# The second layer of a graph network: scalars of x spread by DMA and contracted in one go

## The chip, the cores and the metric

The kernel runs on one core of a Trainium2 chip. The metric is the device time of one execution in microseconds, as a median over runs. The engines are PE (TensorE), DVE (VectorE), ACT (ScalarE), POOL (GpSimd) and SP (SyncE, which here only issues DMAs).

## What is computed

Two layers of a message-passing network over 12500 nodes and 200000 edges, each followed by a layer norm. A node has 160 features: 64 scalars and 32 vectors of three components. The change is in the node update of the second layer:

```
a0, a1 = agg[:, :64], agg[:, 64:].reshape(n, 32, 3)      # sum of the messages at each node
xs, xv = x[:, :64], x[:, 64:].reshape(n, 32, 3)
u0 = einsum('nu,nv,uvw->nw', xs, a0, Wu_ss) * INV64 + einsum('nui,nvi,uvw->nw', xv, a1, Wu_vv) * (INV_SQRT3 * INV32)
u1 = (einsum('nu,nvi,uvw->nwi', xs, a1, Wu_sv) + einsum('nui,nv,uvw->nwi', xv, a0, Wu_vs)) * INV_SQRT2048
u0 = u0 + xs @ Lu_s * INV8
u1 = u1 + einsum('nui,uw->nwi', xv, Lu_v) * INV_SQRT32
x = layernorm(x + x + concat(u0, u1))                    # the layer adds x, and the caller adds x again
```

The first term of u0, with a weight of 64 x 64 x 64, is the one that the change computes in another way. All of it is in f32.

## The kernel before

The program has three stages. The first sorts the edges by their source node and makes the first layer's messages. The second is the first layer's sweep over 100 tiles of 125 nodes, which also makes the second layer's messages. The third is the second layer's sweep over the same tiles (`node_sweep`, `node_step` with `layer == 1`), some 1800 of the 6805 us. There is no scheduler: each engine runs its list as it is written, and they wait for each other on semaphores. A step t sums the messages of tile t (`edges`) and updates tile n = t - 1 (`nodes`). So the engines' work in a step of the second layer is, in each one's order:

- PE: `bilinear(0..5)`, of which 0 to 3 make scalar products into prods_ps (L1301, L1302: 64 rows each, the two halves of the array), each of the two buffers in turn, and 4 and 5 make the mixed products (L1304, L1305); `sum_edges`, the product of the one-hot matrix with the messages (L1352, 17 blocks) and the spilled rows (L1353); `turn_q(0)` (L1339); `scalar_sums`, which adds up zs by products with a band matrix, four groups of 32 columns at a time (L1320); `turn_q(1)`; `turn_y`, which turns the aggregate (a2) and x (x2, v) (L1382 to L1384); `linear`, which adds the linear part, the products of q with w_vv (L1369) and the turned scalars (L1371) in m_ps. An f32 product shows as two records.
- DVE: `scalars(0..3)` multiplies the scalar products by the turned x (zs, L1034), `mixed_mul` (L1071), `mixed_sum` (L1084), then the residual, 2 x on top of m_ps (L1115), and h (L1117).
- ACT: `prods_out` copies the mixed products for POOL (L1593), `deviation` (L1537 to L1543), `features` (L1582 to L1584), `summed` (L1608, L1609), `turned_q(0)` (L1601), `scalars_out` (ss_t, L1636), `turned_q(1)`, `turned_y` (L1626 to L1628), `normal` (L1553), and `one_hot` for the next tile (L1701, L1707).
- POOL: its third of the mixed products (L757), then q of tile t (L731, L766).
- SP: the load of x (L562), of the next tile's messages (msgs, L377) and spilled rows (L588), the stores of out (L397, L398).

PE's edge sum of tile t waits for ACT's one-hot matrix (`hot`); ACT's `summed` waits for the edge sum; POOL's q and the turn of y wait for `summed`. The matrix has one buffer, so that ACT builds it only after the edge sum before.

Of the kernel before, what the change touches and what calls it, by code (L numbers as in the profile page):

```python
# [13 lines left out]
P = 128  # L14
# [44 lines left out]
RS_ALL = R0 + R1 + 1  # L59
# [9 lines left out]
USES = [R0 + d * R1 for d in DIRECT]  # L69


def used(layer, r):

    return r + 1 if r < R0 else R0 + DIRECT[layer] * (r + 1 - R0)
# [23 lines left out]
def build(nc, x, src, dst, attr, weights, out):  # L98
# [37 lines left out]
    x_mid = nc.dram_tensor("x_mid", [N, D], F32).ap()  # L136
    picks_d = nc.dram_tensor("picks", [UNITS, P, UB * P], F32).ap()
    recs_d = nc.dram_tensor("edge_recs", [P, NCH, CB * REC], F32).ap()

    with ExitStack() as whole:  # L140
# [21 lines left out]
        in_order = sb("in_order", [P, S])  # L162
        ones_f = sb("ones_f", [P, P])
# [97 lines left out]
        row_id = q3[:, 0:NCOL]  # L261

# [18 lines left out]
        dma_go, sp_go, edges_clear = sem("dma_go"), sem("sp_go"), sem("edges_clear")  # L281
# [5 lines left out]
        def layer_sems(layer):  # L287
            s = {}
            for n in ("hot", "edges_done", "y_out", "y_turned", "y_turned_out", "prods", "prods_used", "upd", "q_mul", "q_part", "ss_out",
                      "q_turned", "q_turned_out", "lin", "lin_out", "h_ready", "deviation", "inverse", "normed",  # L290
                      "msg", "pay_out", "located",
                      "t_turned", "t_turn_out", "t_mm", "t_out", "first_fill",
                      "sp_ids", "sp_link", "sp_index", "sp_rec", "sp_keys", "sp_tab", "sp_sum", "sp_old", "sp_put", "sp_done"):
                s[n] = sem(f"{n}_l{layer}")
            for n in (("picked", "pick_turned", "pick_out"), ("copied", "mixed_mul"))[layer]:
                s[n] = sem(f"{n}_l{layer}")
            for n in ("msgs_in", "x_in", "stored", "spill_in", "rec_in", "t_stored", "filled"):
                s[n] = [sem(f"{n}{b}_l{layer}") for b in range(2)]
            for n in ("win_in", "scattered"):
                s[n] = [sem(f"{n}{q}_l{layer}") for q in range(4)]  # L300
# [24 lines left out]

        def later(k):
# [23 lines left out]
        def _(sp):  # L350
            def carry():
                sp.sem_inc(sp_go, 1)
# [69 lines left out]
            def load_node_weights(layer):  # L422
# [4 lines left out]
                ss_halves = w["u_ss"].rearrange("v (r h c) -> h v r c", h=2, c=512)  # L427
# [38 lines left out]
            def load_recs(layer, k):  # L466
                c, ck, cb = k
                s = LS[layer]
                if within(c, 2, NCH):
                    if layer == 0:  # L470
# [3 lines left out]
                             ).then_inc(s["rec_in"][cb], 16)  # L474
# [78 lines left out]
            def node_step(layer, k, chunk):  # L553
# [12 lines left out]
                if layer == 1 and within(t, 0, NT - 1):  # L566
# [4 lines left out]
                    load_spilled(layer, later(k))  # L571
                if within(t, 2, NT + 2):
# [10 lines left out]
                if layer == 0 and within(t, 2, NT + 2):  # L583
                    store_table(1, (t - 2, half - 1, b))

            def load_spilled(layer, k):
                t, half, b = k
                sp.dma_start(spill_in[b][:, :], spill_sums[layer][bass.ds(t * HM, P), :]).then_inc(LS[layer]["spill_in"][b], 16)  # L588

            for layer in range(2):  # L590
                s = LS[layer]
                if layer == 1:
                    for b in range(2):
                        sp.wait_ge(LS[0]["stored"][b], 32 * (NT // 2))
                first_msgs(layer)
# [1171 lines left out]
```

## Time and profile before

| what | us |
|---|---|
| time, median of 3 runs (6799.92 to 6801.0) | 6800.83 |
| the profiled execution's own time | 6806.87 |
| its span, first to last instruction | 6805.1 |
| PE busy | 5627.2 (83%) |
| DVE busy | 5466.6 (80%) |
| POOL busy | 5272.0 (77%) |
| ACT busy | 3741.2 (55%) |

The busy shares are means over stages with different limits, so that a change in one stage is read from that stage alone: the stretches of time of the rows below. A record of PE's matmuls shows when it started; records overlap, and a row with a count spans them all. An idle time in brackets is that of the engine just before the row, with what ended it.

### The profile page before, as it was taken

To read this page: it belongs to the slowest core of one execution; us is meant where nothing else is said; L and a number is where in the kernel's file an instruction comes from. 1 tells how busy PE (TensorE), PEld (TensorE's weight loads), DVE (VectorE), ACT (ScalarE), POOL (GpSimd) and SP (SyncE) were. 2 spreads that over 40 slices of the span, in tenths; PEclk is the share of its full clock that TensorE was granted. 3 is DMA by queue.
4 is the path that set the end of the run, shared out by engine and by line. 5 is a ranking of instruction groups with operands and counts; after the bars stand their busy time and mean duration, and the time that the engine had idled before them with its cause. 6 is when DMAs were issued, how large, how long until landed. Compare 5 with 4: busy or idle time off the path is not lost.

```text
span 6805.1 us, 145388 instructions
## 1 busy us (share of the span) xinstructions
PE 5627.2 (83%) x52295; PEld 4582.1 (67%) x52295; DVE 5466.6 (80%) x7299; ACT 3741.2 (55%) x11578; POOL 5272.0 (77%) x4099
## 2 busy tenths in 40 slices
PE   5566666666664799999999999999589999999998
PEld 3455555545554577777777777777467777877877
DVE  6777777777775788888888888888378988998998
ACT  2333333333332566666666666666267777777776
POOL 2777777777777478888888888888768788888887
PEclk6787878888887899999999999999799999999999
DMA  7888888888884377878787878787422222222222
GB/s 222 258 259 259 257 258 263 255 259 256 257 257 145 122 259 261 261 259 262 257 262 256 264 256 263 254 266 255 140 92 93 92 96 98 92 93 101 92 92 74
DMA packets 681148, 1380.99 MB, mean 203 GB/s; under 512 B 106047, under 2 KB 487661, under 8 KB 654447
## 3 DMA queue, kind: packets, MB, share of 16 engines
q1 hardware_dynamic: 527695, 1090.23, 51.0%
q0 software_dynamic: 152736, 281.45, 12.2%
q8 instruction: 418, 6.85, 0.4%
q14 instruction: 299, 2.45, 0.1%
HBM read 587.20 MB, written 784.08 MB: 202 GB/s over the span
## 4 chain that ended last, share of the span: by engine, by line
PE 43%; POOL 16%; DMA 10%; DVE 9%; issue 8%; SPq 8%; ACT 6%; POOLq 0%; DVEq 0%; ACTq 0%
POOL slots L647 12%; PE node_ps L1352 8%; PE prods_ps L1301 8%; DMA slots<-pay,slot_all 5%; DVE zs L1034 4%; PE prods_ps L1304 3%; PE prods_ps L1320 3%; POOL q L704 3%; DMA rec<-edge_recs 3%; PE node_ps L1369 3%; PE m_ps L1369 2%; PE turn_ps L1339 2%; ACT onehot L1701 2%; PE s_ps L1217 2%; SPq L346 2%
## 5 line engine op out<-in xcount | busy, mean ns | idle before, releaser
L647 POOL DMA_INDIRECT slots<-pay,slot_all x3136 | 3263.7, 1041 | 1023.9 <-issue 786.6
L1701 ACT ACTIVATE onehot<-node_iota,msgs 128x125 f32<-128x125 f32 x3400 | 1030.5, 398 | 122.1 <-POOLq L691 122.1
L1352 PEld LDWEIGHTS node_ps<-msgs,onehot 128*125 128x125 f32 x6800 | 932.5, 188 | 139.3 <-issue 98.5
L1352 PE MATMUL node_ps<-msgs,onehot 128*125 128x160 f32 x6800 | 981.1, 303 | 35.8 <-ACT onehot L1707 25.2
L1084 DVE TENSOR_REDUCE upd<-work 125x48 f32<-125x3072 f32 x300 | 1004.0, 3347 | 6.8
L1217 PE MATMUL m_ps<-win,picks_sb 125*128 125x160 f32 x3136 | 666.5, 341 | 390.9 <-ACT pay L1502 381.5
L1071 DVE TENSOR_TENSOR work<-prods_ps,yv 125x1024 f32<-125x1024 f32 x800 | 931.4, 1217 | 64.3 <-PE prods_ps L1305 63.4
L1217 PEld LDWEIGHTS m_ps<-win,picks_sb 125*128 125x128 f32 x3136 | 525.2, 217 | 478.8 <-issue 379.7
L731 POOL TENSOR_TENSOR q<-xt,yv 125x3072 f32<-125x3072 f32 x100 | 547.6, 5476 | 340.4 <-PE turn_ps L1339 322.9
L1034 DVE TENSOR_TENSOR zs<-prods_ps,x_t 128x1000 f32<-128x1000 f32 x400 | 469.6, 1196 | 133.8 <-PE prods_ps L1302 133.8
L1487 ACT COPY picks_sb<-s_ps 125x512 f32<-125x512 f32 x392 | 229.8, 586 | 594.8 <-PE s_ps L1199 521.0
L1034 DVE TENSOR_TENSOR zs<-prods_ps,spill_tab 128x1000 f32<-128x1000 f32 x400 | 469.6, 1196 | 90.2 <-PE prods_ps L1302 90.1
L704 POOL TENSOR_TENSOR q<-xt,yv 125x512 f32<-125x512 f32 x400 | 451.3, 1130 | 94.6 <-PE turn_ps L1339 69.8
L766 POOL TENSOR_TENSOR q<-q 125x1024 f32<-125x1024 f32 x200 | 473.0, 2365 | 15.7
L1301 PE MATMUL prods_ps<-a_t,w_bil 64*128 64x125 f32 x3200 | 439.7, 281 | 22.9 <-DVE zs L1034 20.9
L1301 PE MATMUL prods_ps<-spill_tab,w_bil 64*128 64x125 f32 x3200 | 439.9, 281 | 21.2 <-DVE zs L1034 21.1
L1302 PE MATMUL prods_ps<-spill_tab,w_bil 64*128 64x125 f32 x3200 | 457.3, 284 | 0.0
L1302 PE MATMUL prods_ps<-a_t,w_bil 64*128 64x125 f32 x3200 | 457.0, 284 | 0.0
L1707 ACT ACTIVATE onehot<-onehot,ones_f 128x1375 f32<-128x1375 f32 (+2 forms) x300 | 443.8, 1479 | 3.4
L1185 PE MATMUL prods_ps<-bucket_onehot,after_bf 128*128 128x500 bf16 x392 | 171.0, 436 | 330.1 <-DVE bucket_onehot L900 329.7
L1502 ACT COPY pay<-m_ps 128x320 f32<-128x320 f32 x784 | 331.3, 423 | 185.1 <-PE m_ps L1217 183.0
L1301 PEld LDWEIGHTS prods_ps<-a_t,w_bil 64*128 64x128 f32 x3200 | 385.6, 187 | 63.3 <-DVE zs L1034 31.6
(273 smaller groups left out, 13494.3 us busy)
## 6 DMA issues: line engine op xcount, KB each, us to landing
msgs<-slots SPq DMA_DIRECT2D x200, 1428.0 KB, 6.4
slots<-zero SPq DMA_DIRECT2D x183, 1386.0 KB
win<-table SPq DMA_DIRECT2D x784, 160.0 KB
picks<-picks_sb SPq DMA_DIRECT2D x196, 512.0 KB
picks_sb<-picks SPq DMA_DIRECT2D x196, 512.0 KB
table<-tab SPq DMA_DIRECT2D x200, 350.0 KB
slots<-pay,slot_all POOLq DMA_INDIRECT x3136
spill_in<-spill_sums SPq DMA_DIRECT2D x200, 80.0 KB, 6.0
```

Of the source, the lines that this page charges most:

```text
L647: g.indirect_dma_start(out=slots[layer][:, :], out_offset=bass.IndirectOffsetOnAxis(ap=slot_all[:, j:j + 1], axis=0), in_=pay[q][:, j - UB ...
L704: g.tensor_tensor(q3[0:HM, VV * i + V * u0:VV * i + V * u0 + VV // 2].rearrange("p (u v) -> p u v", v=V), xt[nb][0:HM, S:D].rearrange("p ( ...
L731: g.tensor_tensor(q3[0:HM, VV * i0:].rearrange("p (i u v) -> p i u v", u=V, v=V), xt[nb][0:HM, S:D].rearrange("p (u i) -> p i u", i=3)[:, ...
L766: add = g.tensor_tensor(q3[0:HM, 0:VV], q3[0:HM, 0:VV], q3[0:HM, VV * (j + 1):VV * (j + 2)], ALU.add)
L1034: ve.tensor_tensor(zs[:, r, :, :, :], prods_ps[(nb + r) % 2][:, :].rearrange("p (h c) -> p h c", h=2)[:, :, 0:QUARTER * HM].rearrange("p h ...
L1071: ve.tensor_tensor(wk[:, i, :, :].rearrange("p w (h k) -> p h w k", h=2), prods_ps[(nb + r) % 2][0:HM, :].rearrange("p (h w k) -> p h w k" ...
L1084: ve.tensor_reduce(upd1[:, :, w0:w0 + ROUND // KV], mixed_part(r), AX_X, ALU.add).then_inc(s["upd"], 1)
L1217: mm = te.matmul(to[:, D * j:D * j + D], (pick_b[q] if layer else pick_n[hh])[0:WROWS, P * (2 * p + j):P * (2 * p + j) + P], win[q][0:WROW ...
L1301: te.matmul(to[:, HM * q:HM * q + HM], w.bil[0:S, o:o + P], a2_t[nb][0:S, :], start=True, stop=True)
L1302: mm = te.matmul(to[:, 512 + HM * q:512 + HM * q + HM], w.bil[S:P, o:o + P], a2_t[nb][S:P, :], start=True, stop=True)
L1352: te.matmul(node_ps[0:HM, 0:D], onehot[:, j, :], msgs[b][:, j, 0:D], start=(j == 0), stop=False)
L1701: last = ac.activation(onehot[:, j, :], node_iota[:, :], ACT.Square, bias=msgs[b][:, j, LOCAL:LOCAL + 1], scale=-1.0)
```

## The change

In the second layer the term with Wu_ss is computed from products that are made ahead of the matmul. The first layer's sweep writes the turned scalars of its result to HBM (x0_t, one DMA for each tile). In the second layer SP loads them spread over partitions: partition v of each half holds, for 8 values of u, the row x[u, 125 nodes], the same in all 64 partitions (`spread_x`: four pieces z, two DMAs of 64 x 4000 bytes for each). DVE multiplies each piece in place by the turned aggregate, which it reads from PSUM (`spread_scaled`). PE contracts the 128 rows (u half and v) with the weights of 64 columns, 32 products which alternate between the two halves of the columns and accumulate in node_ps (`scalar_products`); the vv products follow in the same form into the same sum (`vector_products`). ACT copies that sum as ss_t, and one product with `folded` (two identity matrices, one above the other) adds the halves to m_ps. The residual 2 x goes into the linear weights (`ident2` is twice the identity), and the operation for it on DVE is gone. Three of the four pieces have two buffers (in zs, and in parts of pay and picks that the second layer leaves free), the fourth has one. Some semaphores are shared between the layers to make room; the first layer's step is otherwise as before, but for the store of x0_t and a wait of ACT for it ahead of its next copy into ts_t.

The core of the diff:

```
 DVE
+                def spread_scaled(z):
+                    ve.wait_ge(s["y_turned_out"], 3 * n + 3)
+                    if z == 0:
+                        ve.wait_ge(s["xs_in"][nb], 32 * (SPREAD - 1) * (nh + 1))
+                    if z == SPREAD - 1:
+                        ve.wait_ge(s["xs_last"], 32 * n + 32)
+                    ve.tensor_tensor(xs[nb][z][:, :, :], xs[nb][z][:, :, :], s_ps[:, 2 * HM:3 * HM].unsqueeze(1).broadcast_to([P, PER, HM]),
+                                     ALU.mult).then_inc(s["scaled"], 1)
...
-                    for r in range(R0):
-                        scalars(r)
+                    for z in range(SPREAD):
+                        spread_scaled(z)
...
-                    if layer == 1:
-                        ve.scalar_tensor_tensor(m_ps[0:HM, 0:D], xt[nb][0:HM, :], 2.0, m_ps[0:HM, 0:D], ALU.mult, ALU.add).then_inc(s["lin_out"], 1)
-                        ve.wait_ge(s["lin_out"], n + 1)
 PE
+                def scalar_products():
+                    if not nodes:
+                        return
+                    te.wait_ge(s["y_out"], Y_OUT * min(t + 1, NT))
+                    for z in range(SPREAD):
+                        te.wait_ge(s["scaled"], SPREAD * n + z + 1)
+                        for r in range(PER):
+                            o, half_of = S * (PER * z + r), S * (r % 2)
+                            mm = te.matmul(node_ps[half_of:half_of + S, 0:HM], w.bil[:, o:o + S], xs[nb][z][:, r, :],
+                                           start=(z == 0 and r < 2), stop=False, tile_position=(0, half_of))
+                        mm.then_inc(s["scaled_used"], 1)
+                def vector_products():
+                    if not nodes:
+                        return
+                    te.wait_ge(s["q_turned_out"], 2 * n + 2)
+                    for j in range(QC):
+                        half_of = S * (j % 2)
+                        mm = te.matmul(node_ps[half_of:half_of + S, 0:HM], w.vv[:, j, :], q_t[:, j, :],
+                                       start=False, stop=(j >= QC - 2), tile_position=(0, half_of))
+                    mm.then_inc(s["out0"], 1)
...
-                    for r in range(SUMS):
+                    for r in range(R0, SUMS):
                         bilinear(r)
                     sum_edges()
                     turn_q(0)
-                    scalar_sums()
+                    scalar_products()
                     turn_q(1)
                     turn_y()
+                    vector_products()
                     linear()
 ACT
-                    ac.wait_ge(s["prods"], RS_ALL * n + RS_ALL)
+                    ac.wait_ge(*((s["ss_prods"], n + 1) if layer == 0 else (s["out0"], n + 1)))
...
                     turned_q(0)
-                    scalars_out()
                     turned_q(1)
                     turned_y()
+                    scalars_out()
                     normal()
 SP
+                if layer == 1 and within(t, 0, NT):
+                    for z in range(SPREAD):
+                        spread_x(k, z)
...
+                    sp.dma_start(x0_t[t - 2], ts_t[:, :]).then_inc(LS[1]["x_put"], 16)
+            def spread_x(k, z):
+                t, half, b = k
+                s = LS[1]
+                behind = 2 if z < SPREAD - 1 else 1
+                if within(t, behind, NT):
+                    sp.wait_ge(s["scaled_used"], SPREAD * (t - behind) + z + 1)
+                for hh in range(2):
+                    frm = x0_t[t, S // 2 * hh + PER * z:S // 2 * hh + PER * (z + 1), :].rearrange("u n -> (u n)")
+                    sp.dma_start(xs[b][z][S * hh:S * hh + S, :, :].rearrange("p r n -> p (r n)"), frm.unsqueeze(0).broadcast_to([S, PER * HM])
+                                 ).then_inc(s["xs_in"][b] if z < SPREAD - 1 else s["xs_last"], 16)
```

ACT's list in a step of the second layer, from the first copy of q_t to the copies of the mixed products of the next step. Before:

```order
L1601 COPY q_t<-turn_ps 128x500 [waits lin_l1,q_turned_l1]
L1636 COPY spill_tab<-prods_ps 128x125 [waits lin_l1,prods_l1]
L1601 COPY q_t<-turn_ps 128x500 [waits q_turned_l1]
L1626 COPY spill_tab<-s_ps 128x125 [waits lin_l1,y_turned_l1]
L1627 COPY spill_tab<-s_ps 128x125
L1628 COPY spill_tab<-s_ps 96x125
L1553 ACTIVATE res<-centred,stats 125x160 [waits stored1_l1,inverse_l1]
L1701 ACTIVATE onehot<-node_iota,msgs 128x125 [waits edges_done_l1,msgs_in0_l1]
L1701 ACTIVATE onehot<-node_iota,msgs 128x125 x16
L1707 ACTIVATE onehot<-onehot,ones_f 128x2125 [waits squared1]
L1593 COPY pay<-prods_ps 125x1024 [waits mixed_mul_l1,prods_l1] x2
```

And now, the same place:

```order
L1682 COPY q_t<-turn_ps 128x500 [waits out0_l1,q_turned_l1]
L1682 COPY q_t<-turn_ps 128x500 [waits q_turned_l1]
L1707 COPY spill_tab<-s_ps 128x125 [waits lin_l1,y_turned_l1]
L1708 COPY spill_tab<-s_ps 128x125
L1709 COPY spill_tab<-s_ps 96x125
L1717 COPY spill_tab<-node_ps 128x125 [waits lin_l1,out0_l1]
L1634 ACTIVATE res<-centred,stats 125x160 [waits stored1_l1,inverse_l1]
L1782 ACTIVATE onehot<-node_iota,msgs 128x125 [waits edges_done_l1,msgs_in0_l1]
L1782 ACTIVATE onehot<-node_iota,msgs 128x125 x16
L1788 ACTIVATE onehot<-onehot,ones_f 128x2125 [waits squared1]
L1674 COPY pay<-prods_ps 125x1024 [waits mixed_mul_l1,prods_l1] x2
```

The copy of the scalars (L1636, now L1717) went from between the two copies of q_t to just ahead of the normalisation, and waits for `out0`, which PE signals behind the vv products.

PE's list in a step of the second layer, from the turn of y to the turn of q, before (the scalar products of the bilinear part, 32 rows of L1301 and L1302, are left out between the pieces):

```order
L1384 MATMUL s_ps<-ident,yx 96x125
L1366 MATMUL m_ps<-w_lin_u,v_t 125x96 [waits h_ready_l1,q_turned_out_l1]
L1367 MATMUL m_ps<-w_lin,x_t 125x64
L1369 MATMUL m_ps<-w_vv,q_t 125x64 x8
L1371 MATMUL m_ps<-in_order,spill_tab 125x64 [waits ss_out_l1]
L1301 MATMUL prods_ps<-spill_tab,w_bil 128x125 [waits copied_l1,prods_used_l1,y_turned_out_l1]
L1302 MATMUL prods_ps<-spill_tab,w_bil 128x125
```

And now, from the turn of y to the turn of q:

```order
L1462 MATMUL s_ps<-ident,yx 96x125
L1394 MATMUL node_ps<-q_t,w_vv 64x125 [waits q_turned_out_l1]
L1394 MATMUL node_ps<-q_t,w_vv 64x125 x7
L1441 MATMUL m_ps<-w_lin_u,spill_tab 125x96 [waits h_ready_l1]
L1442 MATMUL m_ps<-w_lin,spill_tab 125x64
L1447 MATMUL m_ps<-folded,spill_tab 125x64 [waits ss_out_l1]
L1356 MATMUL prods_ps<-w_bil,x_t 125x512 [waits copied_l1,prods_used_l1,y_turned_out_l1]
L1357 MATMUL prods_ps<-w_bil,a_t 125x512
L1356 MATMUL prods_ps<-w_bil,x_t 125x512 [waits copied_l1,prods_used_l1,y_turned_out_l1]
L1357 MATMUL prods_ps<-w_bil,a_t 125x512
L1426 MATMUL node_ps<-msgs,onehot 125x160 [waits y_out_l1,spill_in1,hot_l1]
L1426 MATMUL node_ps<-msgs,onehot 125x160 x16
```

Between the linear part and the edge sum stood 32 scalar products and the four mixed ones; now the four mixed ones alone do, and the edge sum with its wait for `hot` comes right behind them.

## Rows read from the trace of the kernel before

**Rows 1.** Stretches: us, busy us (records) of PE, PEld, DVE, ACT, POOL, PEclk, DMA, GB/s

```profile
3500.00:4600.00 1100.00, 1051.70 (x10338) 853.96 (x10338) 932.02 (x720) 700.15 (x2371) 914.33 (x845) 1.00 0.80 259
5000.00:6700.00 1700.00, 1611.78 (x19053) 1355.19 (x19052) 1529.43 (x1208) 1280.54 (x3534) 1380.56 (x465) 1.00 0.28 95
```

**Rows 2.** PE's timeline in one step: start us, us, engine, line, operation, tiles

```profile
6038.06 4.88 PE L1352 MATMUL node_ps<-msgs,onehot 128*125 128x160 f32 x34
...
6046.73 0.46 PE L1366 MATMUL m_ps<-w_lin_u,v_t 96*125 96x96 f32 x2 [0.35 <-ACT q_t L1601]
...
6054.19 0.69 PE L1304 MATMUL prods_ps<-w_bil,spill_tab 64*125 64x512 f32 x1 [0.20 <-DVE zs L1034]
...
6056.36 4.88 PE L1352 MATMUL node_ps<-msgs,onehot 128*125 128x160 f32 x34
```

**Rows 3.** Chain of waits in the second layer: start us, us, what

```profile
6043.22 0.43 PE turn_ps L1339 x4
6043.64 1.84 PE prods_ps L1320 x64
6045.48 0.59 PE turn_ps L1339 x4
...
6047.38 1.75 PE m_ps L1369 x16
6049.12 0.22 PE m_ps L1371 x2
```

**Rows 4.** Waits, 5100 to 6600 us: who for whom, us in total, times, longest us

```profile
PE prods_ps L1301 <- DVE zs L1034: 33.5, 82, 0.4
```

**Rows 5.** ACT in the same step, its timeline

```profile
6045.55 0.26 ACT L1636 COPY spill_tab<-prods_ps 128x125 f32<-128x125 f32 x1 [1.29 <-PE prods_ps L1320]
...
6046.88 0.28 ACT L1628 COPY spill_tab<-s_ps 96x125 f32<-96x125 f32 x1
6047.04 0.45 ACT L1553 ACTIVATE res<-centred,stats 125x160 f32<-125x160 f32 x1
6047.37 5.03 ACT L1701 ACTIVATE onehot<-node_iota,msgs 128x125 f32<-128x125 f32 x17
6052.43 2.07 ACT L1707 ACTIVATE onehot<-onehot,ones_f 128x2125 f32<-128x2125 f32 x1
```

**Rows 6.** A gap of PE in the sort: its timeline, and stretches of 1 us

```profile
493.45 0.39 PE L1185 MATMUL prods_ps<-bucket_onehot,after_bf 128*128 128x500 bf16 x1 [4.62 <-DVE bucket_onehot L900]
...
493.00:494.00 1.00, 0.55 (x4) 0.34 (x5) 0.96 (x3) 0.00 (x0) 0.74 (x1) 0.99 0.96 279
494.00:495.00 1.00, 1.00 (x8) 0.98 (x6) 0.93 (x3) 0.00 (x0) 0.96 (x1) 0.50 0.61 196
...
497.00:498.00 1.00, 1.00 (x4) 0.29 (x2) 0.95 (x2) 0.00 (x0) 0.70 (x2) 0.81 1.08 404
```

**Rows 7.** The first two edge sums of the second layer, timeline, and a stretch

```profile
4959.54 7.74 PE L1352 MATMUL node_ps<-msgs,onehot 128*125 128x160 f32 x34 [11.06 <-ACT onehot L1707]
...
4976.42 4.88 PE L1352 MATMUL node_ps<-msgs,onehot 128*125 128x160 f32 x34
...
4959.00:4965.00 6.00, 5.46 (x20) 5.49 (x21) 0.00 (x0) 1.06 (x4) 0.00 (x0) 0.50 0.00 0
```

**Rows 8.** DVE's groups, 5000 to 6700 us: busy us, mean ns, idle before

```profile
L1034 DVE TENSOR_TENSOR zs<-prods_ps,spill_tab 128x1000 f32<-128x1000 f32 x184 | 212.3, 1196 | 20.1 <-PE prods_ps L1302 20.1
L1115 DVE SCALAR_TENSOR_TENSOR m_ps<-xt,m_ps 125x160 f32<-125x160 f32 x93 | 30.7, 330 | 12.8 <-DVE upd L1084 0.5
```

**Rows 9.** DMA issues, 5100 to 6600 us (KB, us to landing), and SP's timeline

```profile
msgs<-slots SPq DMA_DIRECT2D x82, 1428.0 KB, 6.4
...
6050.60 0.43 SPq L377 DMA_DIRECT2D msgs<-slots  x1
```

**Rows 10.** SP's waits in the first layer's sweep, 3000 to 4500 us

```profile
SPq L397 <- ACT tab L1476: 716.4, 58, 13.6
```

**Rows 11.** The last edge sum, PE's timeline

```profile
6770.06 4.88 PE L1352 MATMUL node_ps<-msgs,onehot 128*125 128x160 f32 x34
```

More of the change, by code:

```diff
@@ L68, with used @@
 DIRECT = (3, 2)
-USES = [R0 + d * R1 for d in DIRECT]
-def used(layer, r):
-    return r + 1 if r < R0 else R0 + DIRECT[layer] * (r + 1 - R0)
+USES = [R0 + DIRECT[0] * R1, DIRECT[1] * R1]
+SPREAD = 4
+PER = S // 2 // SPREAD
+def used(r):
+    return r + 1 if r < R0 else R0 + DIRECT[0] * (r + 1 - R0)
 def row_sum(r, half):
@@ L324, in within, with recs_by @@
             return not isinstance(k, int) or lo <= k < hi
+        def recs_by(layer, ck):
+            return 16 * (NCH // 2 * layer + ck + 1)
         def later(k):
@@ L1345, in sum_edges @@
                     te.wait_ge(s["hot"], t + 1)
-                    te.wait_ge(s["spill_in"][b], 16 * half + 16)
+                    te.wait_ge(spill_in_by[b], 16 * (NT // 2 * layer + half + 1))
                     if layer == 0 and within(t, 2, NT):
@@ L1357, in linear @@
                         return
-                    te.wait_ge(s["q_turned_out"], 2 * n + 2)
-                    if layer == 0 and edges:
-                        te.wait_ge(s["y_out"], Y_OUT * t + Y_OUT)
-                    if layer == 1 and within(n, 1, NT):
+                    if layer == 0:
+                        te.wait_ge(s["q_turned_out"], 2 * n + 2)
+                        if edges:
+                            te.wait_ge(s["y_out"], Y_OUT * t + Y_OUT)
+                    elif within(n, 1, NT):
                         te.wait_ge(s["h_ready"], n)
@@ L1367, in linear @@
                     te.matmul(to[0:HM, 0:S], x2_t[nb][:, :], w.lin0[:, :], start=layer == 1, stop=False)
-                    for j in range(QC):
-                        te.matmul(to[0:HM, 0:S], q_t[:, j, :], w.vv[:, j, :], start=False, stop=False)
+                    if layer == 0:
+                        for j in range(QC):
+                            te.matmul(to[0:HM, 0:S], q_t[:, j, :], w.vv[:, j, :], start=False, stop=False)
                     te.wait_ge(s["ss_out"], n + 1)
-                    te.matmul(to[0:HM, 0:S], ss_t[:, :], in_order[:, :], start=False, stop=True).then_inc(s["lin"], 1)
+                    te.matmul(to[0:HM, 0:S], ss_t[:, :], (in_order, folded)[layer][:, :], start=False, stop=True).then_inc(s["lin"], 1)
                 def turn_y():
@@ L1458, in table_turned @@
                     ac.wait_ge(s["t_mm"], m)
+                    if layer == 1:
+                        ac.wait_ge(s["x_put"], 16 * m)
                 ac.copy(ts_t[:, :], turn_ps[0:S, 0:HM])
@@ L1589, in prods_out @@
                         return
-                    ac.wait_ge(s["prods"], RS_ALL * n + R0 + j + 1)
+                    ac.wait_ge(s["prods"], R1 * n + j + 1)
                     if within(n, 1, NT):
                         ac.wait_ge(s["mixed_mul"], R1 * n - R1 + j + 1)
-                    ac.copy(prods_sb[j][0:HM, :], prods_ps[(nb + R0 + j) % 2][0:HM, :]).then_inc(s["copied"], 1)
+                    ac.copy(prods_sb[j][0:HM, :], prods_ps[(R0 + j) % 2][0:HM, :]).then_inc(s["copied"], 1)
                 def turned_q(part):
@@ L1632, in scalars_out @@
                         return
-                    ac.wait_ge(s["prods"], RS_ALL * n + RS_ALL)
+                    ac.wait_ge(*((s["ss_prods"], n + 1) if layer == 0 else (s["out0"], n + 1)))
                     if within(n, 1, NT):
                         ac.wait_ge(s["lin"], n)
-                    ac.copy(ss_t[:, :], prods_ps[(nb + SUMS) % 2][:, 0:HM]).then_inc(s["ss_out"], 1)
+                    ac.copy(ss_t[:, :], (prods_ps[(nb + SUMS) % 2] if layer == 0 else node_ps)[:, 0:HM]).then_inc(s["ss_out"], 1)
                 def normal():
@@ L1731, with laid_out @@
 }
-def laid_out(name, a):
+def laid_out(name, a, layer):
+    if name == "u_ss" and layer == 1:
+        return np.ascontiguousarray(a.transpose(1, 0, 2).reshape(S, SS))
     if name in ("u_ss", "u_vs"):
```

115 lines of the change are left out of this document (69 added, 46 removed).

## The prediction

> **What bounds the kernel now.** I read by stage first [rows 1]. In the stretch from 5000 to 6700 us, which is the second layer's sweep over the nodes, PE is busy 1611.78 of 1700 us, at the full granted clock (1.00), with VectorE (DVE) at 1529.43 behind it; the DMA engines have a share of 0.28 and move 95 GB/s. Only this stage and its loads are touched by most of the change. One step of it is one tile of 125 nodes, and from one edge sum to the next are 6056.36 - 6038.06 = 18.30 us [rows 2]. The chain of waits runs through PE block after block [rows 3], and the longest wait of a PE matmul for another engine is 0.4 us [rows 4].
>
> So a reader may think: take PE work away, and DVE with 1529.43 / 1700 x 18.30 = 16.5 us a step is next. That is only so if no other closed loop is longer than 16.5 us, and the trace of ScalarE (ACT) shows one that now has little slack. In ACT's order the one-hot matrix of the next tile (L1701, L1707) stands behind the copies of this step, runs from 6047.37 to 6052.43 + 2.07 = 6054.50 [rows 5], and PE's edge sum (L1352) waits for it. The next edge sum begins at 6056.36: the one-hot was ready 1.86 us early. The loop edge sum, products, copies, one-hot, next edge sum is thus 18.30 - 1.86 = 16.4 us long today.
>
> **The change part by part.** *PE work.* The 32 bilinear products of 64 rows go, the 64 band records (L1320, 1.84 us) go, and what replaces both is 32 products of 128 rows and 64 columns, f32, thus 64 records, which alternate between the two column halves. No row has this form. The nearest are the band sums: 64 records, four column groups side by side, 1.84 / 16 = 0.115 us for each group of four [rows 3]. With two side by side I take 32 x 0.115 = 3.68 us. The bounds are 1.84 (a record costs the same as there) and 64 x 0.115 = 7.36 (no overlap). I take 3.68, since the moving side has the same 125 columns as the band sums. They stand in the step where the band sums stood, between the two turns of q. The eight vv products change their form likewise: 16 records in pairs, 8 x 0.115 = 0.92 us (bounds 0.46 and 1.84; 1.75 now [rows 3]), and they move out of the linear part to ahead of it.
>
> *ACT's order.* This is the term that decides. ss_t was copied early, between the two copies of q_t, and is now copied behind turned_y from the sum that also holds the vv products. So the scalars' copy, the normalisation, and the one-hot behind it on ACT all wait until PE has done its vv products. New loop, from an edge sum's start: to the start of the scalar products 6043.64 - 6038.06 = 5.58; scalar products 3.68; second turn of q 0.59 [rows 3]; from its end (6045.48 + 0.59 = 6046.07) over ACT's copy of q_t to the first PE instruction that waits for it, 6046.73: 0.66 [rows 2]; vv products 0.92; PE's end to ACT's copy 0.07 (6045.48 to 6045.55), copy to normalisation 0.16 (6046.88 to 6047.04), normalisation to one-hot 0.33 (to 6047.37), together 0.56; one-hot 7.13 [rows 5]; 0.05 for the signal to PE. Sum 19.17 us. That is 0.87 over the present 18.30, although PE has less to do.
>
> *PE's gap and its clock.* From the end of the vv products PE has the linear part left, 6047.38 - 6046.73 = 0.65 and 0.22 of the last product [rows 3], and the mixed products, 6056.36 - 6054.19 = 2.17 [rows 2]. Then it stands until the one-hot is ready: 0.56 + 7.13 - 0.65 - 0.22 - 2.17 = 4.65 us in every step, where its longest wait is 0.4 now. What such a gap does is in the stage of the sort: after 4.62 us without a matmul the granted clock went from full to 0.50, the 1.2 GHz level, and it stayed there from the slice at 494 us through 0.19 / 0.50 = 0.38 of the one at 497, 3.38 us in which PE was busy [rows 6]. At half speed that costs 1.69 us. The edge sum itself shows the far end: behind a long gap, at 0.50, its 34 records took 7.74 us, and 4.88 in the next step [rows 7]: 2.86 us. In the new loop the work right behind the gap is this edge sum, on the path. Bounds 0 (the clock holds) and 2.86; I take 1.69, the gap of the same length. Step: 19.17 + 1.69 = 20.86 us.
>
> *Switches.* The second turn of q takes 0.59 us and the first 0.43, for the same four records [rows 3]: 0.16 us go where the column groups change. The change adds one such place on the loop, ahead of the vv products: up to 0.16 us a step, 98 x 0.16 = 16 us in all. I leave it out of the sum, since the 0.59 that I took already holds one such fill and the block ahead of the vv products is only three turns long, and keep it for the range (19.17 + 0.16 = 19.33). The Trainium skill (TensorEngine Tiling, Key Properties) says that a change of tiling mode drains the engine; by that rule the 16 us would be paid in full, and the 0.16 of the trace agrees with it.
>
> *DVE.* Four zs products of 1000 elements (1196 ns each) become four products in place, one input from PSUM as now; the 330 ns of the residual (L1115) go [rows 8]. So 16.5 - 0.3 = 16.2 us a step. In a step of 20.86 this is hidden; each new product could take 1 us more before DVE set the pace. They wait for the loads and for y_turned; queued behind them are the mixed products, and those wait for ACT's copies of prods_ps, which stand behind the one-hot, so that DVE too idles in the middle of its step. h then follows the linear part, 0.87 us behind the vv products, and PE asks for it a whole step later.
>
> *Loads.* Each step brings 8 DMAs of 64 x 4000 bytes, 2.05 MB, beside the present 95 GB/s x 18.30 us = 1.74 MB. 3.79 MB at the 259 GB/s that the first layer's sweep moves [rows 1] take 14.6 us, under the step. On SP's queue they stand behind the msgs load and ahead of the stores of out and of the next step's loads; 8 x 0.43 [rows 9] is 3.4 us of issue, where SP issues five DMAs a step now. The one-hot needs msgs a step later, which lands in 6.4 us [rows 9]. The fourth piece has one buffer and waits for PE's last scalar product; SP then waits for normed anyway. Price nothing; if the rate were half, 29 us a step.
>
> *The first layer.* One DMA of 32 KB a step on SP, which waits 716.4 us in 58 steps for the table there [rows 10], and a wait of ACT for that DMA a step later: nothing. The fold matrix and the residual in the weights are made once: nothing.
>
> **Sum.** The last edge sum of the sweep begins at 6770.06, the second at 4976.42 [rows 7, 11]: 98 steps of 18.30. 98 x (20.86 - 18.30) = 251 us. The profiled execution takes 6806.87 us (span 6805.1), 6 us above the median of 6800.83; 6806.87 + 251 - 6 = 7052 us.
>
> **Rivals.** (a) *The clock holds at 1.00.* Then the step is 19.17: 98 x 0.87 = 85, thus 6886. For it: the whole sweep is at 1.00 now. Against it: [rows 6]. (b) *Faster.* A record of the new products starts as often as a band record, whatever the number of column halves: scalar products 1.84, vv products 0.46, loop 16.87, and PE's clock holds; 98 x (16.87 - 18.30) = -140, thus 6661, DVE close behind. It decides from the point at which both blocks together take under 4.60 - 0.87 = 3.73 us. For it: records of 29 ns exist [rows 3]. Against it: there four column groups run at once, here two, and the gap for the clock stays. (c) *The two halves do not run side by side.* Blocks of 7.36 and 1.84, step 19.17 + 4.60 = 23.77, thus 7337 with the clock at full and 7503 with the price of the gap. The band sums speak against it, and the Trainium skill (TensorEngine Tiling, Available Configurations and Key Properties) lists 128 x 64 as two tiles that work in parallel; no row here shows it. (d) *The loads set the pace* with many reads of the same bytes: 29 us a step, 7850.
>
> **How the numbers follow.** The forecast, the loop over ACT with a fall of the clock, has 0.72 and reaches from 6930 to 7190 (step 19.6 to 22.2, that is up to 19.33 + 2.86). (a) has 0.12, (b) 0.06, (c) 0.04, (d) 0.04, and 0.02 are left for a step that comes out as now. The range takes in the forecast and (a): 6860 to 7190. Faster by over 0.2% is (b), 0.06; within 0.2% 0.04, the 0.02 and part of (a); slower 0.90. 0.2% is about what a measurement of this kernel can tell from no change.
>
> **What would show it.** Right: PE idle some 4.6 us ahead of each edge sum, released by ACT's one-hot; granted clock under 1.00 in the sweep, with edge sums of 6 to 8 us; steps near 20.9 us; scalar products 3.7 us at full clock; DVE below 85% busy. (a) shows a clock of 1.00 and steps of 19.2; (b) blocks of 1.84 and 0.46; (c) blocks of 7.4; (d) DVE waiting for loads at its first product. The prediction is wrong if ACT's one-hot does not end last ahead of the edge sum.

## The result, and the profile after

The changed kernel takes 7100.77 us (median of 4 runs, 7098.47 to 7103.29) where the kernel before takes 6800.91 beside it: a ratio of 1.044, 95% interval 1.0422 to 1.0458. It is 300 us slower; forecast were 251 us. The profiled execution took 7103.29 us, its span 7101.6.

By stages first, as in [rows 1]: us, busy us (records) of PE, PEld, DVE, ACT, POOL, granted clock, DMA share, GB/s, after the change.

```profile
3500.00:4600.00 1100.00, 1051.78 (x10336) 853.92 (x10334) 932.19 (x719) 699.82 (x2367) 914.12 (x845) 1.00 0.80 261
5000.00:6700.00 1700.00, 1268.67 (x11263) 1093.37 (x11261) 1272.14 (x958) 1079.17 (x3029) 1180.63 (x398) 0.88 0.63 177
```

The first layer's sweep is what it was. In the second layer's sweep every engine is busy for less of the time, PE 75% where it was 95%, and the clock granted to PE is 0.88 where it was 1.00. No engine is the bound; something closes a loop. PE's timeline of one step shows where (line numbers of the changed kernel: L1426 is the edge sum, L1383 the scalar products, L1394 the vv products, L1356 the mixed products). It answers [rows 2].

```profile
6019.35 6.95 PE L1426 MATMUL node_ps<-msgs,onehot 128*125 128x160 f32 x34 [5.00 <-ACT onehot L1788]
...
6027.06 1.93 PE L1383 MATMUL node_ps<-pay,w_bil 128*64 128x125 f32 x32
...
6031.94 1.08 PE L1394 MATMUL node_ps<-q_t,w_vv 128*64 128x125 f32 x16 [0.35 <-ACT q_t L1682]
6032.95 0.46 PE L1441 MATMUL m_ps<-w_lin_u,spill_tab 96*125 96x96 f32 x2
...
6033.75 0.69 PE L1356 MATMUL prods_ps<-w_bil,x_t 64*125 64x512 f32 x1
...
6035.14 0.59 PE L1356 MATMUL prods_ps<-w_bil,x_t 64*125 64x512 f32 x1
...
6040.73 0.63 PE L1426 MATMUL node_ps<-msgs,onehot 128*125 128x160 f32 x1 [5.00 <-ACT onehot L1788]
```

This step lasts 6040.73 - 6019.35 = 21.38 us (18.30 before). The bracket is the reading that matters: PE stood still for 5.00 us ahead of the edge sum, and ACT's one-hot matrix ended that wait; the longest wait before was 0.4 [rows 4]. The view of waits (us in total, times, longest us) from 5100 to 6500 us says that this is so in every step (66 steps, 5.0 us each). DVE does not wait for a load anywhere; its waits are one ahead of its mixed products (L1124) and one ahead of h, for the linear part (L1447):

```profile
PEld node_ps L1426 <- ACT onehot L1788: 384.9, 66, 5.8
PE node_ps L1426 <- ACT onehot L1788: 330.1, 66, 5.0
...
DVE picks_sb L1124 <- issue: 202.6, 66, 3.4
DVE h L1167 <- PE m_ps L1447: 150.2, 65, 3.3
```

For L1124 the view names no releaser. By the kernel it waits for ACT's copy L1674, which stands behind the one-hot in ACT's list, and the timelines of the two engines fit that, since DVE starts as the first of the two copies ends:

```profile
6040.59 1.91 ACT L1674 COPY pay<-prods_ps 125x1024 f32<-125x1024 f32 x2
6041.67 1.23 DVE L1124 TENSOR_TENSOR picks_sb<-prods_ps,yv 125x1024 f32<-125x1024 f32 x1 [3.06 <-issue]
```

The chain of waits (start us, us, what), to be set against [rows 3], runs through ACT for over a third of the step:

```profile
6019.35 6.95 PE node_ps L1426 x34
...
6027.06 3.64 PE node_ps L1383 x64
6030.70 0.59 PE turn_ps L1413 x4
6031.31 0.59 ACT q_t L1682
...
6031.94 1.10 PE node_ps L1394 x16
...
6033.23 0.43 ACT res L1634
6033.65 4.93 ACT onehot L1782 x17
6038.61 2.08 ACT onehot L1788
```

And the clock, in stretches of 1 us around the end of the gap (columns as above; the clock is the third number from the end):

```profile
6039.00:6040.00 1.00, 0.00 (x0) 0.00 (x0) 0.00 (x0) 1.00 (x1) 0.92 (x2) 1.00 0.95 400
6040.00:6041.00 1.00, 0.27 (x1) 0.27 (x2) 0.00 (x0) 1.00 (x2) 1.00 (x1) 0.83 0.92 312
6041.00:6042.00 1.00, 1.00 (x5) 1.00 (x6) 0.33 (x1) 1.00 (x2) 1.00 (x2) 0.50 0.98 230
...
6044.00:6045.00 1.00, 1.00 (x9) 1.00 (x8) 1.00 (x2) 0.73 (x4) 1.00 (x2) 0.96 1.03 244
```

As PE resumes it falls to 0.50, the 1.2 GHz level, and is back at 2.4 GHz three to four us later. The edge sum stands in just that stretch: over the steps from 5100 to 6450 us its 34 records take 6.27 to 7.83 us, 6.89 in the mean, where every one took 4.88 before.

### The profile page after: what moved, and what is told of

Read it like the earlier page. It is cut to its first block, busy times and chain, and to the rows that moved or that the text cites. A ratio compares the mean times of both kernels' runs of the same rounds, so it can differ in the third digit from the quotient of the medians.

```text
span 7101.6 us, 133589 instructions
## 1 busy us (share of the span) xinstructions
PE 5478.5 (77%) x45895; PEld 4487.5 (63%) x45895; DVE 5415.4 (76%) x7200; ACT 3721.0 (52%) x11578; POOL 5268.9 (74%) x4099
## 4 chain that ended last, share of the span: by engine, by line
PE 38%; ACT 16%; POOL 16%; DMA 8%; issue 8%; SPq 8%; DVE 6%; POOLq 0%; DVEq 0%; ACTq 0%
POOL slots L682 13%; PE node_ps L1426 11%; ACT onehot L1782 9%; PE node_ps L1383 5%; PE prods_ps L1353 5%; DMA slots<-pay,slot_all 3%; ACT onehot L1788 3%; DMA rec<-edge_recs 3%; POOL q L739 3%; PE node_ps L1445 2%; PE s_ps L1267 2%; PE turn_ps L1413 2%; SPq L363 2%; SPq L389 2%; ACT q_t L1682 2%
## 5 line engine op out<-in xcount | busy, mean ns | idle before, releaser
L1426 PE MATMUL node_ps<-msgs,onehot 128*125 128x160 f32 x6800 | 1178.6, 341 | 530.7 <-ACT onehot L1788 520.1
L1426 PEld LDWEIGHTS node_ps<-msgs,onehot 128*125 128x125 f32 x6800 | 1130.0, 221 | 641.0 <-ACT onehot L1788 617.1
L1124 DVE TENSOR_TENSOR work<-prods_ps,yv 125x1024 f32<-125x1024 f32 x800 | 931.3, 1217 | 64.7 <-PE prods_ps L1357 63.4
L1124 DVE TENSOR_TENSOR picks_sb<-prods_ps,yv 125x1024 f32<-125x1024 f32 x200 | 235.6, 1220 | 303.9 <-issue 300.5
L1682 ACT COPY q_t<-turn_ps 128x500 f32<-128x500 f32 x400 | 228.6, 572 | 443.6 <-PE turn_ps L1413 441.6
L1689 ACT COPY xa<-node_ps 125x128 f32<-125x128 f32 x200 | 53.3, 267 | 737.7 <-PE node_ps L1427 737.7
L1107 DVE TENSOR_TENSOR q<-q 125x1024 f32<-125x1024 f32 x186 | 234.4, 1260 | 146.9 <-POOL q L739 146.9
L1249 PE MATMUL s_ps<-ident,picks_sb 128*125 128x128 f32 x1568 | 320.5, 338 | 22.0 <-ACT picks_sb L1568 18.4
L1137 DVE TENSOR_REDUCE upd<-picks_sb 125x48 f32<-125x3072 f32 x100 | 334.3, 3343 | 1.1 <-issue 1.1
L1267 PE MATMUL node_ps<-win,picks_sb 125*128 125x160 f32 x1568 | 330.2, 339 | 2.1 <-ACT pay L1583 2.0
```

Source lines behind the costliest of these rows:

```text
L1124: ve.tensor_tensor(wk[:, i, :, :].rearrange("p w (h k) -> p h w k", h=2), prods_ps[((nb if layer == 0 else 0) + r) % 2][0:HM, :].rearrange ...
L1137: ve.tensor_reduce(upd1[:, :, w0:w0 + ROUND // KV], mixed_part(r), AX_X, ALU.add).then_inc(s["upd"], 1)
L1267: mm = te.matmul(to[:, D * j:D * j + D], (pick_b[q] if layer else pick_n[hh])[0:WROWS, P * (2 * p + j):P * (2 * p + j) + P], win[q][0:WROW ...
L1426: te.matmul(node_ps[0:HM, 0:D], onehot[:, j, :], msgs[b][:, j, 0:D], start=(j == 0), stop=False)
L1682: ac.copy(q_t[:, QC // 2 * part:QC // 2 * (part + 1), :], turn_ps[:, 0:QC // 2 * HM].rearrange("p (c n) -> p c n", n=HM)).then_inc(s["q_tu ...
```

## The experiments

**Theory:** the closed loop edge sum, scalar products, vv products, ACT's copy and one-hot, next edge sum sets the step, and its gap on PE costs the clock on top. **Rivals:** the spread transfers or DVE set the pace; the edge sum is slow for another reason than the gap; the loop does not run over the copy of the scalars. Steps and edge sums are means over 5100 to 6450 us of each trace; times are medians, those of the kernel before beside them 6799 to 6803. Each trace is of one run, mostly within 4 us of the median; that of e2_vv_linear took 7013.71 us, that of e1_hot_early 6683.17 and that of e9_before_early 7190.18.

| kernel | time, us | ratio, 95% interval | step, us | edge sum, us | clock, 5100 to 6500 us |
|---|---|---|---|---|---|
| before | 6800.91 | 1 | 18.30 | 4.88 | 1.00 |
| changed | 7100.77 | 1.0422 to 1.0458 | 21.33 | 6.89 | 0.88 |
| e3_fill | 6908.43 | 1.0141 to 1.0175 | 19.33 | 4.88 | 1.00 |
| e4_few_loads | 7100.32 | 1.0424 to 1.0459 | 21.33 | 6.89 | 0.88 |
| e2_vv_linear | 6998.75 | 1.0272 to 1.0306 | 20.48 | 7.00 | 0.88 |
| e5_half_s | 7020.49 | 1.0300 to 1.0334 | 20.48 | 7.75 | 0.83 |
| e1_hot_early | 6693.00 | 0.9834 to 0.9867 | 17.11 | 4.99 | 0.93 |
| e7_msgs_early | 6575.74 | 0.9651 to 0.9683 | 15.97 | 4.88 | 1.00 |

**The clock by itself (e3_fill).** Products of no use in PE's gap; everything else as in the changed kernel:

```diff
+                    if nodes and edges:
+                        if within(n, 1, NT):
+                            te.wait_ge(s["h_ready"], n)
+                        for j in range(6):
+                            te.matmul(m_ps[0:HM, D:512], w.bil[:, 128 * j:128 * j + HM], w.bil[:, 1024:1024 + 512 - D], start=True, stop=True)
                     sum_edges()
```

> The changed kernel with six products of no use (128 x 125 weights, 352 columns, written to columns of a bank that nobody reads) put on TensorE between the mixed products and the edge sum, where it waits 5.0 us for the one-hot matrix; by columns against the 4.88 us of the edge sum's 18 products of 160 they last 6 x 0.59 = 3.5 us, so they fit in the gap. Theory (the clock falls because TensorE stands still in each step, and the slow edge sum then lies on the loop): granted clock over 0.97, edge sums 4.9 to 5.2 us instead of 6.3 to 7.8, step 19.2 to 19.6 us, time 7101 - 99 x 1.9 = 6910 us (6890 to 6950). Rival (edge sums are slow because of the loads' traffic or the operands, or the clock falls for the sum of work): edge sums stay over 6 us, 7090 to 7140 us. Were the products themselves on the path, the time would rise by up to 3.5 x 99 = 350 us.

6908.43 us, as the theory has it. PE's timeline, two steps' ends:

```profile
6000.07 3.81 PE L1472 MATMUL m_ps<-w_bil 128*125 128x352 f32 x12
6005.15 4.88 PE L1426 MATMUL node_ps<-msgs,onehot 128*125 128x160 f32 x34 [1.26 <-ACT onehot L1793]
...
6024.47 0.81 PE L1426 MATMUL node_ps<-msgs,onehot 128*125 128x160 f32 x4 [1.25 <-ACT onehot L1793]
```

PE does 3.8 us more work in each step and the kernel is 192 us faster. ACT's one-hot still ends the wait, so the loop is the same; the edge sum is back at 4.88 us in every step and the clock at 1.00. The loop at full clock is 19.33 us, and the clock costs 21.33 - 19.33 = 2.00 us a step, which is what the edge sum lost (6.89 - 4.88 = 2.01). (The expectation took 0.59 us for a product, from 18 products in 4.88 us; the 34 records of that row are 17 products, which makes 4.88 / 17 x 352 / 160 = 0.63, and six of them the 3.8 us that were measured.)

**The loads (e4_few_loads).** The destination of each spread transfer is cut to 2 of 64 partitions, and the multiplication is replaced by the larger of the two:

```diff
-                    sp.dma_start(xs[b][z][S * hh:S * hh + S, :, :].rearrange("p r n -> p (r n)"), frm.unsqueeze(0).broadcast_to([S, PER * HM])
+                    sp.dma_start(xs[b][z][S * hh:S * hh + 2, :, :].rearrange("p r n -> p (r n)"), frm.unsqueeze(0).broadcast_to([2, PER * HM])
...
-                                     ALU.mult).then_inc(s["scaled"], 1)
+                                     ALU.max).then_inc(s["scaled"], 1)
```

> The changed kernel, with each of the eight spread transfers of a tile writing 2 partitions instead of 64, so that 1/32 of 1 MB is written for each tile (62 of 64 partitions keep old numbers: this part of the computation is left out; VectorE takes the larger of the two numbers instead of the product so that they stay bounded, with the same operands and sizes). Theory (the transfers are hidden and take nothing from the engines): no change, 7085 to 7115 us, step 21.3 us, edge sums still 6.3 to 7.8 us. Rival (the transfers' traffic slows edge sums, messages or VectorE): the step falls by 0.5 to 2.5 us, 6850 to 7050 us.

7100.32 us, the same steps and the same edge sums. The stretch shows that the bytes did go, the share of the DMA engines from 0.63 to 0.25:

```profile
5100.00:6500.00 1400.00, 1045.79 (x9278) 902.76 (x9280) 1047.44 (x787) 888.67 (x2488) 971.54 (x330) 0.88 0.25 84
```

So the bytes of the spread cost nothing here, neither as a wait nor through other engines' speed. The eight issues of a step are still in this kernel; that they cost nothing is not shown apart.

**The vv products and the copy behind them (e2_vv_linear).** Of the change, the placing of the vv products is undone, and with it the place of ACT's copy:

```diff
                     turn_y()
-                    vector_products()
                     linear()
...
                     turned_q(0)
+                    scalars_out()
                     turned_q(1)
                     turned_y()
-                    scalars_out()
```

> One part of the change undone: the products of the vector pairs stand in the linear part again, as in the kernel before, instead of being added to the scalar sums, so that ScalarE's copy of the scalars waits for the scalar products alone and stands ahead of its second copy of q. Theory (loop over ScalarE): from the end of the scalar products to the first one-hot activation 2.86 us now, of which 1.10 us of vector products and the copy behind them (0.26) give way to the copies of the turned features (0.57): 0.8 us less, so that the step is 20.4 to 20.6 us and the time 7101 - 99 x 0.8 = 7020 us (7000 to 7060), with the clock little changed. Rival (the loop does not run over the copy of the scalars; VectorE or the loads set the pace): no change, 7085 to 7115, or slower by the products that now stand ahead of the sum of h.

6998.75 us, at the low end of what was expected (just under it): the step lost 0.85 us, near the 0.8 read from ACT's timeline, and the clock stayed. The wait for the vv products was on the loop. Without the clock's price the loop lost 0.96, since the edge sum became 0.11 longer (7.00). PE's gap is shorter here, 3.73 us where it was 5.00, since the vv products now stand in the linear part:

```profile
6012.76 7.45 PE L1426 MATMUL node_ps<-msgs,onehot 128*125 128x160 f32 x34 [3.73 <-ACT onehot L1789]
```

So the length of the gap alone does not set what the clock costs.

**Half of the scalar products (e5_half_s).**

```diff
-                        for r in range(PER):
+                        for r in range(PER // 2):
                             o, half_of = S * (PER * z + r), S * (r % 2)
```

> The changed kernel with every second pair of scalar products left out on TensorE (32 of 64 for each tile: half of that sum is not computed); the spread transfers, VectorE's four multiplications and everything else stay. Theory (the scalar products lie on the loop that sets the step): they last 1.8 us instead of 3.64, the step falls by 1.8 us to 19.5 us with the gap before the edge sum unchanged at 5.0 us and the clock as low as it was, time 7101 - 99 x 1.8 = 6920 us (6890 to 6950). Rival (VectorE or the transfers, which do the same work, set the step, or the products lie beside something else): no change, 7085 to 7115 us.

7020.49 us: 80 us less, not 180. The rival (no change) is out, but the theory's number is wrong too, in one assumption, that the clock stays as it was. PE's timeline:

```profile
6003.30 7.75 PE L1426 MATMUL node_ps<-msgs,onehot 128*125 128x160 f32 x34 [5.00 <-ACT onehot L1788]
...
6011.82 1.93 PE L1383 MATMUL node_ps<-zs,w_bil 128*64 128x125 f32 x32
...
6023.78 7.74 PE L1426 MATMUL node_ps<-msgs,onehot 128*125 128x160 f32 x34 [5.01 <-ACT onehot L1788]
```

The block went from 3.64 to about 1.8 on the loop, the gap is the same 5.00, but the edge sum now takes 7.75 us in every step, 0.86 over the mean of the changed kernel: 21.33 - 1.8 + 0.86 = 20.4, and 20.48 was measured. Nearly half of what the shorter block saved went back through the clock.

**ACT's order (e1_hot_early).** The one-hot of the next tile begins as soon as the edge sum is read:

```diff
                     summed()
                     turned_q(0)
+                    if nxt:
+                        distances(1, later(k), 0, 12)
                     turned_q(1)
                     turned_y()
+                    if nxt:
+                        distances(1, later(k), 12, BLOCKS)
                     scalars_out()
+                    if nxt:
+                        selections(1, 2 * t + 4, 0, BLOCKS).then_inc(s["hot"], 1)
                     normal()
-                    if within(t, 0, NT - 1):
-                        one_hot(later(k))
```

> Only ScalarE's order in the second layer's sweep is changed: the one-hot matrix of the next tile is begun as soon as the edge sum is read, 12 of its 17 activations beside the scalar products, 5 behind the copies of the turned features, its last activation (2.07 us) ahead of the normalisation. TensorE, VectorE and GpSimd do the same work in the same order. Theory (the closed loop over ScalarE sets the step, and its gap on TensorE costs the clock): the loop becomes 4.9 + 0.4 + 4.2 + 0.6 + 1.1 + 1.5 + 0.3 + 2.1 = 15.1 us, below VectorE's own 16.0 us of work, so that the step falls from 21.3 to 16.3 to 17.0 us, the gap before the edge sum to under 2.5 us, the granted clock rises over 0.95, and the time is 7101 - 99 x 4.3 to 5.0 = 6605 to 6675 us, faster than the kernel before. Rival one (the spread loads or VectorE's waits set the pace of 21 us): no change, 7080 to 7120. Rival two (only the clock is slow, for another reason than the gap): the step loses the 3.5 us of one-hot hidden beside the products at most but keeps edge sums of 7 us, 6740 to 6850 us.

6693.00 us: faster than the kernel before, but above 6605 to 6675. The step is not even, 14.89 to 20.9 us. Its waits from 5100 to 6500 us:

```profile
PE node_ps L1394 <- ACT q_t L1682: 118.6, 82, 3.8
...
ACT onehot L1787 <- DMA msgs<-slots: 101.1, 61, 3.7
PEld node_ps L1426 <- ACT onehot L1793: 39.6, 52, 0.8
```

and those of SyncE's own queue, where L414 is the store:

```profile
SPq L414 <- ACT res L1634: 454.6, 82, 8.0
```

The wait for the one-hot is nearly gone (39.6 us where it was 384.9 for the same weight loads), and a new one stands behind it: ACT now asks for the messages earlier than they come. PE feels it at the second copy of q, which stands behind the twelve activations in ACT's list: it waits 118.6 us there. Some of the table's clock of 0.93 stands behind these waits: in the step at 6008 us PE waited 1.98 us, and then its mixed products took 1.06 us each, where they take 0.59 at full clock, and the edge sum 5.83. Their load is queued on SP behind the store, and the store waits for the normalisation, which had been moved behind the one-hot. The expectation had not looked at that queue.

**The message load (e7_msgs_early).** In addition, on SP:

```diff
-                if layer == 1 and within(t, 0, NT - 1):
-                    if within(t, 1, NT):
-                        sp.wait_ge(s["edges_done"], t)
-                        if within(t, 1, NT - 1):
-                            load_msgs(layer, later(k))
-                    load_spilled(layer, later(k))
                 if layer == 1 and within(t, 0, NT):
                     for z in range(SPREAD):
+                        if z == SPREAD - 1 and within(t, 0, NT - 2):
+                            sp.wait_ge(s["edges_done"], t + 1)
+                            load_msgs(layer, later(later(k)))
+                            load_spilled(layer, later(later(k)))
                         spread_x(k, z)
...
-                if layer == 0:
-                    load_spilled(layer, (1, 0, 1))
+                load_spilled(layer, (1, 0, 1))
```

> The version with the one-hot matrix begun early (6693 us), and in addition SyncE's message load for the tile after next is issued as soon as the edge sum has freed its buffer, ahead of the last spread transfers and of the store, where it stood behind a wait for the residual row and the normalised tile. In that version ScalarE waited 101 us for the messages between 5100 and 6500 us. Theory (after the loop over ScalarE, the messages come last in every third or fourth step, and behind them VectorE's own 16.2 us of work): no wait for messages is left, the step is 16.2 to 16.7 us, time 6693 - 99 x 0.5 to 1.0 = 6595 to 6645 us. Rival (the loop over ScalarE and the clock are still the bound and the messages are late only because the step is): 6680 to 6700 us.

6575.74 us, ratio 0.9667 to the kernel before. No wait for messages is left, and the stretch now has a bound of the plain kind, DVE busy for 1388.13 of 1400 us, with the clock at 1.00:

```profile
5100.00:6500.00 1400.00, 1252.24 (x12377) 1033.49 (x12378) 1388.13 (x1051) 1180.16 (x3335) 1303.08 (x438) 1.00 0.85 237
```

PE's wait for the second copy of q is 30.4 us, 0.3 each time. The time came 20 us under the expectation. DVE's 16.2 us held four products that stood apart in the kernel before, 4 x 1.196 = 4.78 us [rows 8]; now they run back to back and overlap at their ends, four in 4.51 us (from 6022.61 us in this trace). The step is 15.97.

**That with the vv products in the linear part (e8_msgs_vv):** e2's edit on top of e7's.

> The same as the one with the early message load, and the vector products put back into the linear part, so that ScalarE copies the scalars right behind the scalar products. Theory (VectorE's own work of 16.2 us a step is the bound by then): the same time as the kernel with the early message load, within 15 us. Rival (the chain of scalar sums to h and from there to VectorE's next multiplications is still last in some steps): 20 to 80 us faster than it.

6575.63 us (0.9648 to 0.9681): the same. What was worth 0.85 us a step on the loop is worth nothing where DVE is the bound.

**The message load alone (e11_msgs_alone):** SP's edit without ACT's.

> The changed kernel with the early message load alone; the one-hot matrix stands where the change has it. Theory (the messages are there long before ScalarE is free for them at a step of 21.3 us, so the load matters only once the loop over ScalarE is shortened): no change, 7085 to 7115 us. Rival (the messages, or what stands behind them in SyncE's queue, take part in the step already): 6950 to 7060 us.

7102.47 us (1.042 to 1.0455): nothing, as expected. The load matters only once the loop over ACT is shorter.

**The same order in the kernel before (e9_before_early, e10_before_six).** Are the two edits of order worth as much without the change? The first try kept the 12 activations ahead of the second copy of q:

```diff
                     turned_q(0)
+                    if nxt:
+                        distances(1, later(k), 0, 12)
                     scalars_out()
                     turned_q(1)
                     turned_y()
```

> The kernel before, with the same two edits of order and nothing of the change: the one-hot matrix begun as soon as the edge sum is read (12 of 17 activations ahead of the copy of the scalars, the rest and the last one ahead of the normalisation) and the message load of the tile after next issued right behind the edge sum. Theory (before, TensorE had work for the whole time in which ScalarE builds that matrix, and its longest wait was 0.4 us): no change beyond 0.3%, 6780 to 6820 us. Rival (the loop over ScalarE set the step before too): faster by more than 1 us a step, under 6700 us.

7180.31 us (1.0531 to 1.0566), 377 us slower where no change was expected. PE's wait from 5100 to 6500 us:

```profile
PE m_ps L1363 <- ACT q_t L1598: 127.3, 63, 2.0
```

and the clock from 6009 us on, in stretches of 1 us:

```profile
6009.00:6010.00 1.00, 0.00 (x0) 0.00 (x0) 1.00 (x1) 1.00 (x5) 1.00 (x1) 1.00 0.98 411
6010.00:6011.00 1.00, 0.88 (x8) 0.88 (x9) 1.00 (x1) 1.00 (x6) 1.00 (x1) 1.00 0.26 79
6011.00:6012.00 1.00, 1.00 (x8) 1.00 (x7) 0.09 (x1) 1.00 (x4) 1.00 (x1) 0.62 0.06 16
...
6017.00:6018.00 1.00, 1.00 (x14) 1.00 (x12) 0.49 (x2) 0.00 (x0) 1.00 (x1) 0.50 0.00 0
```

Before the change the scalar sums last 1.84 us [rows 3], not 3.64, so 12 activations of 0.29 us end too late and PE waits 2.0 us a step for the copy queued behind them. That, and PE at 0.50 from 6011 into 6018 us, makes the step 22.13 us. With 6 activations there:

> The kernel before with the two edits of order again, but only 6 of the 17 one-hot activations ahead of the copy of the scalars (1.75 us, for scalar sums that last 1.84 us before, where the changed kernel's scalar products last 3.64), so that the second copy of q is not queued behind them. Theory (in the try with 12, TensorE waited 2.0 us a step for that copy and its clock fell in what followed; without that wait TensorE has work all the time, as before): 6785 to 6815 us, no wait of TensorE over 0.6 us, clock as in the kernel before. Rival (the order of the message load, or the later normalisation, is what cost the 380 us): 7100 us or more.

6803.48 us, ratio 1.000 (0.999 to 1.001); PE's longest wait is again 0.4 us and the clock 1.00. So the order by itself, in this split, gives the kernel before nothing, and the 377 us came from the split into 12, not from the load or the normalisation. The gain of e7 needs both the change (less work on PE) and the order.

## Why the prediction was right, point by point

**The loop over ACT, right.** The prediction's step at full clock was 19.17 us; e3_fill measured 19.33. By pieces, from the chain: scalar products 3.64 (3.68 forecast), second turn 0.59 (0.59), to the vv products 6031.94 - 6031.29 = 0.65 (0.66), normalisation and one-hot 6040.69 - 6033.23 = 7.46 (0.33 + 7.13 = 7.46). The 0.05 for the signal to PE, for which the prediction names no row, is 6040.73 - 6040.69 = 0.04 here. The piece that was off is the vv products, 1.10 where 0.92 was forecast: eight pairs by 0.115 counts from start to start, and the copy behind them also waits for the last pair to end. From the edge sum's start to the scalar products it is 0.07 more (6010.80 - 6005.15 = 5.65 in e3_fill), in the scalar products and in ACT's copies 0.04 less each.

**The price of the clock, right in kind, too small.** 1.69 us were taken from one gap in the sort; 2.00 were measured, within the bounds 0 and 2.86. That is the step of the sum that was mis-sized: 0.31 of the 0.47 us by which the step was longer than forecast (21.33 against 20.86), the loop's 0.16 the rest. 0.47 x 98 = 46 us of the 49 by which 7052 fell short. A single gap could not tell the mean: after the same 5.00 us of standing still the edge sums take between 6.27 and 7.83 us. Nor does the length of the gap, by which the prediction picked its row, settle the price: 3.73 us in e2_vv_linear cost 7.00 - 4.88 = 2.12, and 5.00 us in e5_half_s 2.87. That 1.69 came near was partly luck.

**The gap, nearly.** 5.00 us where 4.65 were forecast: the mixed products run from 6033.75 to 6035.73, 1.98 us, where 2.17 were taken from a row in which they had waited for DVE, and behind the vv products the linear part is 0.71 where 0.87 were taken.

**The switch, open.** The 0.16 us kept for the range are not seen ahead of the vv products: PE stood there 0.35 us waiting for the copy of q. The Trainium skill (TensorEngine Tiling, Key Properties) says that a change of tiling mode drains the engine; with PE already idle, this run shows it neither way.

**DVE and the loads, right.** DVE is busy 1272.14 / 1700 = 75% (under 85 forecast), and e4 shows the bytes to cost nothing. That 16.2 us a step would be next is shown by e7: 15.97.

**The rivals.** (a), the clock holds, did not happen; e3_fill is the same loop with the clock held, at 6908, where 6886 was worked out. (b) and (c) fall by 3.64 us for the block: two column halves run side by side, and each pair costs what four band records did (3.64 / 32 = 0.114 us, 1.84 / 16 = 0.115). (d) falls by e4. What the prediction did not ask is whether the order on ACT has to stay as it is. In this order the new products are part of the slow loop: leaving half of them out took 1.8 us off it (e5), and the wait for the vv products is worth 0.85 us a step (e2). With the one-hot and the message load moved, the same products make a kernel that is faster than the one before (e1, e7).

## What to carry to other kernels

When work is taken from the busiest engine, write down the closed loop of the step that is next, with the instruction that each in-order engine executes last in it: here PE lost work and the loop over ACT, which nobody had had to hide, became the step. Here the gap on PE had a second price in the work right behind it, the clock's 2.00 us a step, so look for both; fillers of no use separate the two prices in one run. When a loop is shortened, look at each queue for the load whose time was given by the old step.

## What the runs showed that was not expected

- Work of no use made the kernel faster: 3.8 us of products a step, 192 us less. (The expectation of e3_fill had it, once the gap had been seen.)
- The price of the gap is not a constant. With the same 5.00 us of standing still, the edge sum took 6.89 us in the mean, and 7.75 in each step once half of the scalar products were left out; after 3.73 us (e2_vv_linear) it took 7.00.
- A gap of 2.0 us (e9_before_early) was followed by a longer stretch at 0.50 than one of 5.0: from the slice at 6011 us, over 1 us after PE had resumed, into that at 6018, against 6040 to 6044 in the step of the changed kernel shown above. With 1.26 us in each step (e3_fill) the clock stayed at 1.00. What decides between these is not settled by these runs.
